# Two attention layers of a Flamingo block: product in one run, two-chunk steps in layer 1, keys in an order that makes a stack row contiguous

## The reference, cut to what matters

```python
# layer 0
q = (query @ Wq.T).reshape(B, Nq, 2 * H, HD).transpose(0, 2, 1, 3)
k = (key_ @ Wk.T).reshape(B, Nk, 2 * H, HD).transpose(0, 2, 1, 3)
v = (value @ Wv.T).reshape(B, Nk, H, 2 * HD).transpose(0, 2, 1, 3)
attn = sdpa(q1, k1, v) - lam * sdpa(q2, k2, v)      # then RMS norm, @ Wp.T + bp
# layer 1
q, k, v = split(query @ Wq.T + bq), split(key @ Wk.T + bk), split(value @ Wv.T + bv)
scores = jnp.einsum('bhqd,bhkd->bhqk', q, k) / jnp.sqrt(HD)
scores = jnp.where(mask[:, None, :, :], jnp.finfo(scores.dtype).min, scores)
ctx = jnp.einsum('bhqk,bhkd->bhqd', softmax(scores), v)
```

## Time and profile before

| | |
|---|---|
| median of 3 runs | 2350.72 us (2350.26 to 2360.24) |
| the profiled execution | 2361.65 us |
| its span, first to last instruction | 2359.2 us |
| mean granted clock of PE | 0.946 |
| PE busy | 2192.7 us, 93% |
| DVE, ACT, POOL busy | 71%, 64%, 54% |
| DMA | 227.82 MB in 113421 packets |

### The profile page before, as it was taken

One profiled execution on the slowest core, in us unless ns is written; L12 is line 12 of the kernel. 1 busy time (PEld: TensorE's weight loads), 2 busy tenths in 40 slices (PEclk: granted clock), 3 DMA queues, 4 the chain that ended last, 5 costly groups with the idle time before them and its releaser, 6 DMA issues. The chain is left out here.

```text
span 2359.2 us, 67435 instructions
## 1 busy us (share of the span) xinstructions
PE 2192.7 (93%) x27256; PEld 1303.0 (55%) x27256; DVE 1677.1 (71%) x3697; ACT 1507.8 (64%) x2133; POOL 1278.9 (54%) x1418
## 2 busy tenths in 40 slices
PE   4799999999999999999967957999999999999798
PEld 3255555555555555555536843666655666666576
DVE  3688888888888888888816555777766677774644
ACT  2177788777877778778763322767666667766322
POOL 5335655655654554655333445777766777762232
PEclk8599999999999999999997975999999999999699
DMA  3635344344444444444201027667665666661100
GB/s 105 128 77 113 96 98 109 101 94 108 106 97 99 112 96 95 115 93 94 48 7 57 24 61 149 137 142 137 143 131 120 127 144 140 138 126 24 54 1 16
DMA packets 113421, 227.82 MB, mean 97 GB/s; under 512 B 46052, under 2 KB 58596, under 8 KB 112612
## 3 DMA queue, kind: packets, MB, share of 16 engines
q1 hardware_dynamic: 113124, 223.67, 42.8%
HBM read 146.77 MB, written 76.48 MB: 95 GB/s over the span
## 5 line engine op out<-in xcount | busy, mean ns | idle before, releaser
L1061 ACT ACTIVATE probs<-score_ps 125x896 f32<-125x896 f32 x1152 | 1014.3, 915 | 210.3 <-PE score_ps L954 207.9
L1119 DVE TENSOR_REDUCE max_part<-max_ps 112x1 f32<-112x500 f32 x1024 | 654.7, 668 | 115.3 <-PE spare_ps L923 68.3
L970 PE MATMUL acc_ps<-probs,vext 125*32 125x224 f32 (+1 forms) x12288 | 673.2, 316 | 6.6 <-issue 6.1
L923 PE MATMUL max_ps<-kstack,qstack 48*112 48x500 f16 x1535 | 508.1, 405 | 4.9 <-DVE max_part L1119 2.6
L954 PE MATMUL score_ps<-qstack,kstack 50*125 50x224 f16 (+1 forms) x6144 | 454.8, 244 | 17.2 <-ACT probs L1061 13.9
L954 PEld LDWEIGHTS score_ps<-qstack,kstack 50*125 50x125 f16 x6144 | 344.4, 134 | 183.8 <-issue 122.2
L1116 DVE CUSTOM_DVE_ANT_0 kstack<-max_ps,kstack 112x500 f32<-112x500 f32 x511 | 335.3, 675 | 134.2 <-PE max_ps L923 80.1
L1119 DVE TENSOR_REDUCE max_part<-spare_ps 112x1 f32<-112x500 f32 x512 | 343.3, 670 | 64.6 <-PE max_ps L923 63.5
L970 PEld LDWEIGHTS acc_ps<-probs,vext 125*32 125x32 f32 x12288 | 261.7, 109 | 225.8 <-issue 156.5
L923 PE MATMUL spare_ps<-kstack,qstack 48*112 48x500 f16 x769 | 310.7, 404 | 20.2 <-issue 16.9
L923 PEld LDWEIGHTS max_ps<-kstack,qstack 48*112 48x112 f16 x1535 | 173.5, 129 | 143.4 <-issue 77.7
(11 more groups left out here) (200 smaller groups left out, 2697.8 us busy)
## 6 DMA issues: line engine op xcount, KB each, us to landing
kstack<-k_parts SPq DMA_DIRECT2D x384, 187.5 KB, 6.6
k_parts<-khl SPq DMA_DIRECT2D x128, 375.0 KB, 2.8
ctx_f<-in_ctx SPq DMA_DIRECT2D x32, 750.0 KB
ctx_f<-context_parts SPq DMA_DIRECT2D x32, 750.0 KB, 4.4
context_parts<-ctx_f SPq DMA_DIRECT2D x16, 750.0 KB, 3.8
context_parts<-kstack SPq DMA_DIRECT2D x16, 750.0 KB, 3.5
mask_in<-in_mask SPq DMA_DIRECT2D x128, 82.0 KB
qrows<-q_parts SPq DMA_DIRECT2D x384, 7.0 KB, 7.0
```

What stands on the lines that cost most here:

```text
L923: nc.tensor.matmul(room(("P", n, p))[0:PIECE, 0:TK], qstack[n % SLOTS][rows, c, PIECE * i:PIECE * (i + 1)], kstack[n % SLOTS][rows, c, TK ...
L970: last = nc.tensor.matmul(acc_ps[32 * j:32 * j + 32, TT * S * i:TT * S * (i + 1)].rearrange("p (s c) -> p s c", s=S), vext[n % SLOTS][:, t ...
L1061: nc.scalar.activation(probs[t % 2][:, 896 * h:896 * h + 896].rearrange("k (b c) -> k b c", b=2), score_ps[(t * H + h) % 2][0:KT, :, 0:448 ...
L1119: nc.vector.reduce_max(best, scores, AX.X).then_inc(s_red, 1)
```

## The change

- `weigh` is one run of all matmuls of a step; where it stands between scores and search is chosen by `order_of` from four orders, three of which are in use: both scores first if the step before had no user but A or M; in layer 1, scores apart by a pair if this step has none; else scores apart by the product.
- Layer 1 has 6 steps of two chunks (`steps`). A step has two scores and two exponentials, as in layer 0, and 4 search pieces; the product of both chunks is one run of 16 matmuls. `AHEAD` is 3 of these steps. Its users now use the score banks, up to two a step, and F is one user with 4 transposes.
- `key_order` permutes the columns of the key projection's weights (and, by eight DMAs from ACT's queue, the key bias) so that the four groups c of one dimension d are neighbours in the stored keys: `(c d)` becomes `(d c)`, and a fill's source row is one run of 12000 bytes where it was four of 3000.
- In layer 1, SP loads the next context after `fill_m` and waits for both mask conversions before the next mask; POOL makes `mask_add` before `mask_f`.

```diff
-        self.uses_f = 2
+        self.uses_f = self.halves
+        self.steps = NKT if self.halves == 2 else NKT // 2
...
+def key_order(layer, weight, *parts):
+
+    if layer == 0:
+        weight = halves_first(weight)
+        rows = [weight[:, r, :, :].rearrange("p h (e d) -> p h e d", e=2) for r in range(2)]
+        parts = [[x[:, HALF * r:HALF * r + HALF].rearrange("p (d h e) -> p h e d", h=2, e=2) for r in range(2)] for x in parts]
+    else:
+        rows = [weight[:, HALF * r:HALF * r + HALF].rearrange("p (c d) -> p c d", c=PAIRS) for r in range(2)]
+        parts = [[x[:, HALF * r:HALF * r + HALF].rearrange("p (d c) -> p c d", c=PAIRS) for r in range(2)] for x in parts]
+    return [(rows[r], *(x[r] for x in parts)) for r in range(2)]
...
+        key_bias = [(columns[HALF * r + c:HALF * (r + 1):PAIRS, 2:4],
+                     a["columns"][HALF * r + HALF // PAIRS * c:HALF * r + HALF // PAIRS * (c + 1), :]) for r in range(2) for c in range(PAIRS)]
...
-        where = {("V", 0): (0, 2), ("F", 0): (1, 2), ("V", 1): (2, 2), ("F", 1): (3, 2), ("V", 2): (4, 2), ("K", 0): (5, 2),
-                 ("K", 1): (6, 2), ("M", 0): (7, 2), ("K", 2): (8, 2), ("A", 0): (10, 2)}
+        where = {("F", 0): (1, 1), ("V", 0): (1, 0), ("V", 1): (2, 0), ("V", 2): (2, 1), ("M", 0): (3, 1), ("K", 0): (3, 0),
+                 ("K", 1): (4, 0), ("K", 2): (4, 1), ("A", 0): (5, 1)}
...
-    AHEAD = 5
+    AHEAD = 3 if L.masked else 5
...
+    ORDERS = {"both scores first": ("scores 0", "scores 1", "pair 0", "weigh", "pair 1", "prepare"),
+              "scores apart by a pair": ("scores 0", "pair 0", "scores 1", "weigh", "pair 1", "prepare"),
+              "scores apart by the product": ("scores 0", "pair 0", "weigh", "scores 1", "pair 1", "prepare"),
+              "pairs apart by preparation": ("scores 0", "weigh", "scores 1", "pair 0", "prepare", "pair 1")}
+
+    def order_of(n, t):
+
+        busy = [any(kind not in "AM" for kind, _, _ in at_step(*place)) for place in ((n, t), (n, t - 1) if t else (n - 1, STEPS - 1))]
+        if not busy[1]:
+            return ORDERS["both scores first"]
+        if L.masked and not busy[0]:
+            return ORDERS["scores apart by a pair"]
+        return ORDERS["scores apart by the product" if L.masked and busy[0] else "scores apart by the product" if busy[0] else "scores apart by the product"]
...
-                                         .rearrange("b (c d) k -> (b d) c k", c=PAIRS)).then_inc(s_ks[n % SLOTS], 16)
+                                         .rearrange("b (d c) k -> (b d) c k", c=PAIRS)).then_inc(s_ks[n % SLOTS], 16)
...
+                    sp.wait_ge(s_big, n)
...
-                    if L.masked:
-                        next_context(n + 4)
...
+                    if L.masked:
+                        next_context(n + 4)
                     store_k(n + 3)
...
-            def weigh(n, t, i):
...
+            def weigh(n, t):
+
+                pe.wait_ge(s_exp, (n * STEPS + t + 1) * 2)
...
+                chunks = [(t, 0)] if H == 2 else [(2 * t + h, 896 * h) for h in range(2)]
+                for chunk, column in chunks:
+                    for i in range(2):
+                        for j in range(4):
```

More of the change, by code:

```diff
@@ L134, in build @@
         rows = sb("rows", [128, sum(ROWS.values())])
-        columns = sb("columns", [128, 2])
-        small = {**unpacked(wide, WIDE), **unpacked(rows, ROWS), "subln": columns[:, 0:1], "bk1": columns[:, 1:2]}
+        columns = sb("columns", [128, 4])
+        small = {**unpacked(wide, WIDE), **unpacked(rows, ROWS), "subln": columns[:, 0:1], "bk1": columns[:, 3:4]}
         tg = small["gates"]
@@ L490, in attend @@
     layer = 0 if L is L0 else 1
-    GD, GC, H = L.group_dims, L.group_cols, L.halves
+    GD, GC, H, STEPS = L.group_dims, L.group_cols, L.halves, L.steps
     K_WORDS = PAIRS * SK
@@ L575, in attend, with at_step @@
     LEAD = {"T": 3, "K": 3, "V": 2, "M": 1, "F": -1, "A": -1}
-    def at_step(n, t, side):
-        return [(kind, n + LEAD[kind], i) for (kind, i), place in where.items()
-                if place == (t, side) and 0 <= n + LEAD[kind] < B]
+    def at_step(n, t):
+        return [(kind, n + LEAD[kind], i) for (kind, i), (step, _) in where.items()
+                if step == t and 0 <= n + LEAD[kind] < B]
     def searched(n, t, k):
-        if 2 * k >= per_step:
-            return []
-        d, place = (1, early + t * per_step) if t < NKT - AHEAD else (2, (t - NKT + AHEAD) * per_step)
+        d, place = (1, early + t * per_step) if t < STEPS - AHEAD else (2, (t - STEPS + AHEAD) * per_step)
         return [("P", n + d, place + 2 * k + r) for r in range(2)] if n + d < B else []
@@ L592, in attend @@
     for n in range(B):
-        for t in range(NKT):
-            middle, last = at_step(n, t, 1), at_step(n, t, 2)
-            spare_uses += middle + last
-            if H == 2:
-                in_scores.update({user: n * NKT + t for user in middle})
-                middle = []
-            order += searched(n, t, 0) + middle + searched(n, t, 1) + last
+        for t in range(STEPS):
+            spare_uses += at_step(n, t)
+            in_scores.update({user: n * STEPS + t for user in at_step(n, t)})
+            order += searched(n, t, 0) + searched(n, t, 1)
     order += [(kind, B - 1, i) for kind, i in turnaround]
@@ L606, in halves_of @@
     def halves_of(step):
-        return (0, 1) if step % 2 == 0 or H == 1 else (1, 0)
+        return (0, 1) if step % 2 == 0 else (1, 0)
     def room(user):
@@ L943, in scores @@
                         pe.wait_ge(s_big, n + 1)
-                buf = score_ps[(t * H + h) % 2]
-                keys = slice(KT * t, KT * t + KT)
+                buf = score_ps[h]
+                chunk, columns = (t, range(h * 2, h * 2 + 2)) if H == 2 else (2 * t + h, range(PAIRS))
+                keys = slice(KT * chunk, KT * chunk + KT)
                 if L.masked:
@@ L949, in scores @@
                                          big_eye[HALF * r:HALF * r + SQ, :], start=True, stop=False, skip_group_check=True)
-                here = PAIRS // H
-                for k in range(here):
+                for k, c in enumerate(columns):
                     for r in range(2):
                         rows = slice(HALF * r, HALF * r + KROWS + 2)
-                        last = nc.tensor.matmul(buf[0:KT, r, GC * k:GC * (k + 1)], kstack[n % SLOTS][rows, h * here + k, keys],
-                                                qstack[n % SLOTS][rows, h * here + k, :], start=not L.masked, stop=True,
+                        last = nc.tensor.matmul(buf[0:KT, r, GC * k:GC * (k + 1)], kstack[n % SLOTS][rows, c, keys],
+                                                qstack[n % SLOTS][rows, c, :], start=not L.masked, stop=True,
@@ L1050, in drain @@
                         at_least(act, s_attn, n)
[L1051 removed]
+                    dst, part = (turned[:, i, :], spare_ps[0:SQ, :]) if H == 2 else (
+                        turned[:, :, 0:256], spare_ps[0:SQ, :].rearrange("q (i x) -> q i x", i=2))
+                    nc.scalar.activation(dst, part, ACT.Copy).then_inc(s_turned, 1)
                 if kind == "A":
@@ L1070, in _ @@
             for n in range(B):
-                for t in range(NKT):
-                    for h in range(H):
-                        exps(n, t, h)
+                for t in range(STEPS):
+                    for place in range(2):
+                        exps(n, t, place)
                     if t == 0 and n:
                         copy_output(n)
-                    for user in at_step(n, t, 1) + at_step(n, t, 2):
+                    for user in at_step(n, t):
                         drain(user)
@@ L1150, in _ @@
             for n in range(B):
-                for t in range(NKT):
+                for t in range(STEPS):
                     for user in searched(n, t, 0):
                         reduce_piece(user)
-                    for user in at_step(n, t, 1):
-                        drain(user)
-                    if t == where["F", 1][0] + 1 and n:
+                    if t == where["F", L.uses_f - 1][0] + 1 and n:
                         reciprocals(n)
```

118 lines of the change are left out of this document (52 added, 66 removed).

## The result

| | before | changed | |
|---|---|---|---|
| median of 3 runs | 2350.72 us | 2417.04 us | ratio 1.0271, 95% interval 1.0246 to 1.0296 |
| span of the profiled execution | 2359.2 | 2416.4 | +57.2 |
| layer 0, one batch (mean of the starts of the copy into `out_sb`) | 35.01 | 34.08 | -0.9 |
| layer 1, one batch, 27 starts | 22.99 | 25.84 | +2.9 |
| layer 1, first to last of the 32 copies | 697.3 | 775.6 | +78.3 |

The kernel became 2.7% slower, where 2283 us had been forecast. Layer 0 moved as forecast, layer 1 went the other way.

What follows compares the result with a forecast made beforehand. PE was taken to bound both layers' attentions. Layer 0 -21, layer 1 -49 and setup +2 gave 2293.7 us against the profiled execution, 2283 against the median; its own range was 2245 to 2310, widened to 2245 to 2400 for rival 1.

Steps and rivals of the forecast that it cites:

- The product in one run: Layer 0: 16 records in one run hold PE 0.89 us, where two halves cost 1.03.
- the floor by the exponential: Layer 0: a step can't be shorter than 2.86 us, since the next first scores wait for this step's second exponential.
- the sum: Whole kernel: -21 for layer 0, -49 for layer 1, +2 for setup; 2283 us against the median.
- The rival of nothing in layer 0: Layer 0: second scores behind the product cost more latency, its 21 us are gone, 2304; chance 0.09 including a softer floor.
- PE's batch in layer 1: Layer 1: PE's batch falls from 22.3 to 20.6 us, by 0.9 from product runs and 0.8 from score banks.
- The stack row of 12000 bytes: Layer 1 fills: longer source rows cut transfer from 8.9 us to 6, the middle of bounds 8.9 and 3.2.
- the loop: Layer 1, search through keys and fill to search: 23.0 us with fills as before, 20.1 with 6 us of transfer.
- the point of decision: Layer 1 fills: 6.5 us of transfer, or 177 GB/s, decides whether the loop fits PE's 20.6 us batch.
- rival 1: Layer 1: fill keeps its rate, PE waits every batch; 2352 if clock holds (chance 0.12), 2439 if it falls (0.16).
- Rival 2: PE's instructions delayed by longer packets on the same DMA engines: +50 us, 2333; chance 0.08.

Runs made afterwards that it cites:

- half the fill's bytes: Changed kernel, but layer 1's fills move only two of four column groups from batch 3 on (results wrong): 2252.73 us, ratio 0.9575.
- striped rows: Changed kernel with each layer 1 fill written to every third partition instead of 16 neighbours: 2295.5 us, ratio 0.9748; also combined with other kernels.
- filler work: Changed kernel plus 14 matmuls without result per layer 1 batch, ahead of the wait for the stack: 2373.31 us, ratio 1.0101.
- keys first: Changed kernel with layer 1's key projections in steps 1 and 2, values in 3 and 4, key store ahead of context load: 2311.01 us, ratio 0.9807.
- keys in the middle: Changed kernel with layer 1's V0 in step 1, K0 and K1 in step 2, K2 in step 3, V1 and V2 in step 4: 2475.47 us, ratio 1.0509.

## Why the prediction was wrong

**Layer 0: right.** The product in one run (0.89), the floor by the exponential (2.86) and its releaser came out as worked out. 34.3 us a batch had been forecast, 34.08 came; in the runs the layer's order alone is worth 24.5 us, where 21 had stood in the sum. The rival of nothing in layer 0 falls.

**PE's batch in layer 1: right in kind, 0.5 us too long.** 20.6 us had been forecast. With half the fill's bytes it is 20.10.

**The stack row of 12000 bytes: this step failed.** The prediction had the loop at 23.0 us with fills as before, and named 6.5 us of transfer, 177 GB/s, as the point of decision. It then took 6 us, the middle between a bound set by the destination (8.9) and one set by the stores (3.2), "since one has the destination and the other the freedom from it". The bounds were not equal. Between the fills and the stores in the earlier trace rows the run length was the same, 3000 bytes, and the partitions were not, so those rows already told which of the two acts. The key order changes only what they have in common. Measured: 128 GB/s with long runs, 129 with short ones, no difference to the time with the order taken out or put in alone, and from the destination alone 163 GB/s over whole batches for 122, or 195 in the best window shown. So the term of 6 us stayed near 9 (9.4 us by the fills' own packets), and PE had a wait in every batch that the sum had at nothing.

The Trainium skill ("SBUF — State Buffer", "Door 1: The DMA port swizzle") has 16 neighbouring partitions on 4 of 16 ports, and partitions 32 apart on the same port; it does not name the row's length there. The traces agree in that the partitions set the rate and the length does not. An estimate from this mapping, one fill after the other: 16 neighbours put 4 rows on each of their ports, so the three fills of a half take 12 row times; 16 striped rows put at most 3 on one port, so the three take 9. That is a factor of 1.33, and 9.4 and 7.1 us are a factor of 1.3, where the expectation had said twice. The fit is one of two numbers; no run varies the load of a port by itself, so the ports as the reason are argued and the partitions are shown. The page's figure for 4 ports, 104 GB/s, lies below the 122 of the fills' packets. The prediction had named the page as speaking against its 6 us and left it to rival 1.

**The loop, term by term.** Forecast 6.0 + 3.3 + 2.9 + 10.8 = 23.0. In the changed kernel's batch: from the waiting pair at 1705.16 to the start of the last K, 1713.6 (half way through the group at 1712.93), 8.5; to the end of its cast 3.2 (1716.82); to the first fill 2.9; from there to the next waiting pair at 1730.92, 11.2. Sum 25.8. Three terms held within 0.4 us; the first is 2.5 longer because much of this stretch runs at half clock. At full clock the loop was seen at 23.0 to 23.3.

**Rival 1 is what happened**, in its sharper form: up to 3 us more a batch by the clock, 2439 us; measured 2417, above the end of the stated range, 2400. It had a chance of 0.16. It is a loop that feeds itself: PE waits, the clock falls, the K projections stand in the slow stretch, the next stack comes later. The filler work cuts it at the clock and is worth 44 us; the striped rows cut it at the fill and are worth 121.

**Rival 2, instruction supply,** is not what slows the changed kernel, which has no such wait in the 500 us. But such stalls are in the kernel before: 7.2 us put down to issue, with falls of the clock, and they went when the fills were made faster. That they come from instructions queued behind data on the DMA engines is not shown. For it: none with striped rows in the steps of before, and most, 14.0 us, where context load and fills lie together. Against it: none in the changed kernel, whose fills are as slow as before, and with keys first the striped rows have 4.7 us for 3.0. The cause stays open.

**The sum.** In spans, -68 had been forecast and +57 came, a miss of 125 us. Layer 1 alone is -49 against +78, 127 us. The 49 themselves were counted from 22.3 us, the period of the first 12 copies; over 27 it was 22.99 with its stalls, and with half the fill's bytes layer 1's copies take 612.3 us for 697.3, 85 less.

## What to carry to other kernels

When two rows of a trace (here stores and fills) differ in rate, ask what differs between them before pricing an edit: an edit that changes only what they share cannot move the one towards the other. For transfers into few neighbouring partitions, try spreading the rows over the tile before lengthening them: here the first was worth 121 us and the second nothing. When a schedule is shortened, write down the loops that run through DMA (last use, projection, split, store, fill, first use) and hold their length against the new period; then check in what order one in-order queue issues the loop's DMAs and those beside it, since that order alone was worth 155 us here.

## What the runs showed of the hardware

- Six fills of 16 rows of 12000 bytes are no faster than six of 16 rows of four runs of 3000: from first issue to last landing 11.3 us (the changed kernel) and 11.6 (the same with runs of 3000).
- The same bytes into every third partition of 48 take 9.0 us; the fills' packets alone go from 122 to 163 GB/s. The issue on SP is dearer: 0.59 us a DMA (median), against 0.42.
- Each of the changed kernel's 19 waits on PE (2.3 to 5.1 us) came with a stretch at a granted clock of 0.5. With striped rows, 4 of 20 waits (0.4 to 2.3 us) did. With filler work, waits of at most 1.2 us were left and the clock still fell in 7 batches of about 20, so the length of the last wait alone does not tell.
- A store of 128 partitions that lands 3.1 us after its issue takes 6.8 when the context load is issued 0.4 us ahead of it (medians of the changed kernel and of the keys in the middle).
